# Setup work of the first phase put in another order: taps, LoRA B products, weight lo parts, and two bias loads

## The reference, cut to what matters

```
agg_w = einsum('bk,koi->boi', softmax(...), weight)
y     = einsum('boi,bih->boh', agg_w, x) + agg_b
z     = y @ A_eff.T,  A_eff = einsum('bn,nri->bri', gate, lora_A)   # and A_shared
x    += y @ kernel + bias + z @ B_eff.T                              # and B_shared
```

## Time and profile before

| what | us |
|---|---|
| three runs | 838.28, 838.53, 830.34 |
| the profiled execution, its own time | 831.89 |
| span of the profiled execution | 829.8 |
| TensorE busy in the span | 786.4 |
| VectorE, ScalarE, GpSimd busy | 532.7, 208.1, 88.3 |

### The profile page before, as it was taken

The page is one execution under the profiler, slowest core; times in us unless marked ns, Lnnn a source line. Parts: engine busy times, 40 slices in busy tenths (PEclk is TensorE's granted clock), DMA queues, the critical chain, the costliest instruction groups (busy, mean ns, idle before and its releaser), DMA issues.

```text
span 829.8 us, 10413 instructions
## 1 busy us (share of the span) xinstructions
PE 786.4 (95%) x3889; PEld 659.2 (79%) x3889; DVE 532.7 (64%) x634; ACT 208.1 (25%) x251; POOL 88.3 (11%) x59
## 2 busy tenths in 40 slices
PE   5998889999999999789999999999999989999998
PEld 4867678888888999668888877877778868888886
DVE  4855775264443479987777759766665795565552
ACT  4431101010010032233333326332233641111110
POOL 4440532323222000000000000000000000000000
PEclk9999999999999999899999999999999999999999
DMA  8966845455455896244455232277754764444441
GB/s 277 238 180 188 216 109 132 122 119 135 111 143 127 199 279 194 70 126 127 126 159 145 76 127 77 64 200 206 203 163 177 271 236 152 153 152 152 167 161 76
DMA packets 88379, 131.45 MB, mean 158 GB/s; under 512 B 11208, under 2 KB 66936, under 8 KB 85656
## 3 DMA queue, kind: packets, MB, share of 16 engines
q1 hardware_dynamic: 85136, 129.90, 53.4%
q10 hardware_dynamic: 3064, 0.90, 0.7%
q0 software_dynamic: 144, 0.21, 0.1%
HBM read 78.20 MB, written 51.72 MB: 157 GB/s over the span
## 4 chain that ended last, share of the span: by engine, by line
PE 72%; DVE 10%; DMA 8%; SPq 5%; issue 3%; ACT 2%; DVEq 0%; ACTq 0%
PE ps L1561 30%; PE ps L1804 25%; PE ps L1862 16%; DMA w_raw<-in_L_ffn_w 2%; DVE cr L1279 1%; DVE cf L1271 1%; SPq L438 1%; DMA w_scratch<-w_d 1%; SPq L592 1%; DMA x<-x_scratch 1%; DVE w_s_lo L1252 1%; DMA lora_b_scratch<-lb_c_lo 1%; DMA h_f<-h_scratch 1%; SPq L355 1%; DMA res<-r_scratch 1%
## 5 line engine op out<-in xcount | busy, mean ns | idle before, releaser
L1804 PE MATMUL ps<-cr,w_s_hi 128*128 128x512 f32 x512 | 159.5, 393 | 5.1 <-ACT s L915 4.9
L1804 PE MATMUL ps<-cr,w_a_hi 128*128 128x512 f32 x384 | 122.2, 400 | 10.7 <-DVE s L1357 6.0
L1804 PEld LDWEIGHTS ps<-cr,w_s_hi 128*128 128x128 f32 x512 | 96.5, 189 | 27.2 <-issue 4.0
L1804 PE MATMUL ps<-cr,w_s_lo 128*128 128x512 f32 x256 | 100.2, 391 | 0.0
L1804 PEld LDWEIGHTS ps<-cr,w_a_hi 128*128 128x128 f32 x384 | 73.3, 192 | 28.4 <-DVE s L1357 8.1
L1561 PE MATMUL ps<-wk_hi,y_hi 128*128 128x512 f32 x256 | 80.5, 395 | 0.3 <-issue 0.3
L1561 PE MATMUL ps<-wk_lo,y_hi 128*128 128x512 f32 x256 | 79.0, 390 | 0.0
L1561 PE MATMUL ps<-wk_hi,y_lo 128*128 128x512 f32 x256 | 78.9, 389 | 0.0
L1127 DVE TENSOR_TENSOR x_t<-ps,x_t 128x1024 f32<-128x1024 f32 x16 | 19.6, 1222 | 92.3 <-PE ps L1561 92.3
L741 POOL TENSOR_TENSOR x_t<-x_in,f_bias 128x1024 f32<-128x1024 f32 x16 | 63.3, 3960 | 143.0 <-DMA x_scratch<-x_t 143.0
L1499 DVE TENSOR_TENSOR res<-ps,res 128x512 f32<-128x512 f32 x56 | 38.6, 689 | 59.0 <-PE ps L1862 58.3
(11 more groups left out here) (176 smaller groups left out, 1255.4 us busy)
## 6 DMA issues: line engine op xcount, KB each, us to landing
x_scratch<-x_t SPq DMA_DIRECT2D x128, 64.5 KB, 2.1
x<-x_scratch SPq DMA_DIRECT2D x32, 258.0 KB, 7.4
x_in<-in_x SPq DMA_DIRECT2D x16, 512.0 KB, 5.3
r_scratch<-r_t SPq DMA_DIRECT2D x16, 512.0 KB, 3.1
raw<-in_L_ffn_w SPq DMA_DIRECT2D x64, 128.0 KB, 4.7
h_scratch<-s SPq DMA_DIRECT2D x32, 256.0 KB, 2.4
h_f<-h_scratch SPq DMA_DIRECT2D x8, 1024.0 KB, 5.9
res<-r_scratch SPq DMA_DIRECT2D x16, 512.0 KB, 5.0
```

The source lines that it names most:

```text
L1804: last = pe.matmul(o, l, r, start=first and q == 0 and n == 0, stop=q == 3 and n == 2, skip_group_check=True)
```

## The change

1. `wpad` is made on VectorE ahead of the four `mix_t` copies, `turn_taps` follows the first y on TensorE, and ScalarE copies the taps after LoRA A's first hi part.
2. LoRA B's products move forward on TensorE: results 0 and 1 ahead of u's step 3, results 2 and 3 ahead of step 4.
3. `POOL_WK` shrinks from (0, 1, 2) to (0,): VectorE makes seven lo parts. The lo parts of LoRA B move ahead of those of weight rows 6 and 7.
4. ScalarE issues the eight b12 loads after y's splits of tile 3, not between the hi parts of weight rows 5 and 6.
5. Three buffers change places: LoRA B's first lo tile to 90 KB, the b3 row to 199.75 KB, the first r tile to 90 KB. So the b3 load waits for weight row 7's slot and stands behind `first_group_lb` in SyncE's queue, and ScalarE waits for the r stores before it writes convolution parts.

```diff
-                for n, ks in (("hi", (162.25, 186.25)), ("lo", (199.75, 203.75)))]
+                for n, ks in (("hi", (162.25, 186.25)), ("lo", (90, 203.75)))]
...
-        r_t = [at(f"r_t{s}", [P, NL], 199.75 + 4 * s) for s in range(2)]
-        b3_s = at("b3_s", [P, NL], 90)
+        r_t = [at(f"r_t{s}", [P, NL], k) for s, k in enumerate((90, 203.75))]
+        b3_s = at("b3_s", [P, NL], 199.75)
...
-        POOL_WK = (0, 1, 2)
+        POOL_WK = (0,)
...
             load_wk(7)
-            wait_slot(sp, raw_of(5))
-            sp.dma_start(b3_s[:, :], b3.partition_broadcast(P)).then_inc(b3_in, 16)
             sp.wait_ge(lbs_made, 2)
...
             first_group_lb(sp, 0)
+            wait_slot(sp, raw_of(7))
+            sp.dma_start(b3_s[:, :], b3.partition_broadcast(P)).then_inc(b3_in, 16)
             sp.wait_ge(lora_taken, N_LORA)
...
             la_hi_part(0)
+            act.wait_ge(taps_mm, 1)
+            for half in range(2):
...
+            last.then_inc(taps_made, 1)
             split_y(1, 0, 1)
...
                 act.dma_start(f_bias[:, :], f0_bias.partition_broadcast(P)).then_inc(fbias_in, 16)
-                for m in range(4):
-                    for h in range(2):
-                        act.dma_start(b12_s[32 * m:32 * m + 32, h, :],
...
             wk_hi_part(6)
             wk_hi_part(7)
-            act.wait_ge(taps_mm, 1)
...
             split_y(3, 1, 1)
+            with nc.allow_non_contiguous_dma(reason="a few columns of small arrays"):
+                for m in range(4):
+                    for h in range(2):
+                        act.dma_start(b12_s[32 * m:32 * m + 32, h, :],
...
+            act.wait_ge(r_stored[0], 16 * TILES // 2)
...
+            dve.wait_ge(wpad_zeroed, 1)
+            dve.wait_ge(small_in, 48)
+            dve.tensor_copy(wpad[:, 8:8 + TAPS, :], w9_raw[:, :, :].rearrange("o c k -> o k c")).then_inc(wpad_made, 1)
             for q in range(4):
...
             y_rest(0, 0, 0)
-            dve.wait_ge(wpad_zeroed, 1)
-            dve.wait_ge(small_in, 48)
-            dve.tensor_copy(wpad[:, 8:8 + TAPS, :], w9_raw[:, :, :].rearrange("o c k -> o k c")).then_inc(wpad_made, 1)
+            wk_lo_part(1)
...
-            take_y(1, 0, 1)
+            add_bias(1)
+            wk_lo_part(2)
+            y_rest(1, 0, 1)
             wk_lo_part(3)
...
             wk_lo_part(5)
+            for n in range(4):
+                lb_lo_part(n)
             wk_lo_part(6)
             wk_lo_part(7)
-            for n in range(4):
-                lb_lo_part(n)
...
             y_tile(0, 0, 16, True)
+            turn_taps()
             small_turns()
...
             first_u(0, 1)
+            pe.wait_ge(taps_made, 1)
             la_result(2)
...
                 first_u(1, k)
-            for k in range(3, 5):
-                dst, dst1 = first_u(0, k), first_u(1, k)
-            turn_taps()
             lb_result_mm(0)
             lb_result_mm(1)
-            dst, dst1 = first_u(0, 5), first_u(1, 5)
-            pe.wait_ge(taps_made, 1)
+            dst, dst1 = first_u(0, 3), first_u(1, 3)
+            pe.wait_ge(lora_taken, 4)
             lb_result_mm(2)
             lb_result_mm(3)
-            for k in range(6, 8):
+            for k in range(4, 8):
                 dst, dst1 = first_u(0, k), first_u(1, k)
```

More of the change, by code:

```diff
@@ L833, in _ @@
             la_hi_part(0)
+            act.wait_ge(taps_mm, 1)
+            for half in range(2):
+                last = act.activation(taps[:, :, half, :].rearrange("p g (q o) -> p g q o", q=PH),
+                                      bank(6 + half).rearrange("p (q g o) -> p g q o", q=PH, g=GRP), ACT.Copy)
+            last.then_inc(taps_made, 1)
             split_y(1, 0, 1)
@@ L844, in _ @@
                 act.dma_start(f_bias[:, :], f0_bias.partition_broadcast(P)).then_inc(fbias_in, 16)
-                for m in range(4):
-                    for h in range(2):
-                        act.dma_start(b12_s[32 * m:32 * m + 32, h, :],
-                                      b12.rearrange("(h m j b) -> h m b j", h=2, m=4, j=NJ)[h, m]).then_inc(b12_in, 16)
             wk_hi_part(6)
             wk_hi_part(7)
-            act.wait_ge(taps_mm, 1)
[L852 to L855, removed]
             for n in range(4):
@@ L860, in _ @@
             split_y(3, 1, 1)
+            with nc.allow_non_contiguous_dma(reason="a few columns of small arrays"):
+                for m in range(4):
+                    for h in range(2):
+                        act.dma_start(b12_s[32 * m:32 * m + 32, h, :],
+                                      b12.rearrange("(h m j b) -> h m b j", h=2, m=4, j=NJ)[h, m]).then_inc(b12_in, 16)
             for k in range(4, 6):
@@ L1632, in turn_taps @@
                 pe.wait_ge(wpad_made, 1)
-                pe.wait_ge(lora_taken, 4)
                 for half in range(2):
```

## The result

The changed kernel takes 829.41 us (median of 20 runs, 825.13 to 831.96), the kernel before on the same chips 833.55 us (20 runs, 828.3 to 838.53). The ratio is 0.9945, with a 95% interval of 0.9926 to 0.9964: 4.6 us faster by the ratio, 4.1 by the medians, where the forecast was 1.9 us slower and 837 us. One execution in this document, the third of run e10, took 2783 us and is left out of that run's numbers. The profiled execution's own time is 827.55 us, against 831.89 before.

The account below looks back on a forecast made before the run. TensorE was taken as the bound, busy 786.4 of 829.8 us, with at most 12.3 us to win in three waits. Landing +0.9 and clock +1.0 gave +1.9 us on 834.8, so 837 us, range 827 to 844.

Parts of the forecast that it names:

- Early work: Moved taps and weight lo parts before about 61 us: hidden behind TensorE's work, taken as 0, bounds 0 and +1 us.
- LoRA B's lo parts about 6 us earlier: On VectorE, LoRA B's last lo part is made at 48.4 us, against 54.45 before.
- Wait 1: TensorE's 3.04 us wait for group 0's LoRA B copies goes, with its low clock: u of tile 2 ends 4.7 us earlier.
- Wait 2: TensorE's 2.77 us wait for group 1's LoRA B grows to 8.3 us; the last store lands 0.9 us later.
- +1.4 for the start: Term of the stores' landing: the DMA work from x of tile 3 on starts 1.4 us later, 49.7 against 48.34.
- "-2.2" for the copies: Term of the stores' landing: shared LoRA B copies finished before and ScalarE's copies ahead by 1.2 us, estimated at -2.2 us.
- rival C: Queues run freely: the last store lands at 72.5 us, wait 3's low clock goes; -8.1 us, 827 us; chance 0.10.
- Behind it: After wait 2 the clock falls; y of tile 4 comes 2 us later, about half returns: +1.0 us.
- wait 3: TensorE's 3.2 us "issue" wait for VectorE's y lo parts: forecast to stay at 2.5 us, its 1.6 us low clock too.
- B: Issues decide: landing 1.6 us earlier, VectorE 1.0 later, wait 3's low clock gone; -2.2 us, 833 us; chance 0.20.
- D: Slower: b3 ahead of the stores costs 4.8 us, later start, b12 and clock the rest; +8.2 us, 843 us; chance 0.12.
- E: ScalarE's group 0 copies queue behind the x loads and wait 1 stays; +0.9 us, 836 us; chance 0.08.

Follow-up runs that it names:

- e10: Changed kernel with GpSimd's first x plus bias of the loop held until VectorE has made y of tile 4 with its bias; 832.38 us, ratio 1.0006.
- e1: Changed kernel with the weight lo parts of k = 1 and 2 back on GpSimd; 829.26 us, ratio 0.9938 to the kernel before.
- e7: Changed kernel with LoRA B's four lo parts again behind those of weight rows 6 and 7 on VectorE; 828.53 us, ratio 0.9945.
- e2: Changed kernel with the b3 load behind the eight LoRA B stores in SyncE's queue; 829.58 us, ratio 0.9941 to the kernel before.
- e6: Changed kernel with LoRA B's DRAM laid out so each store has 64 rows of one stride, not 8 blocks of 8; 827.62 us, ratio 0.9907.
- e8: The e6 kernel plus GpSimd's third x plus bias held until VectorE has made y's lo parts of tile 5; 823.81 us, ratio 0.9902.
- e3: Kernel before with only GpSimd's x plus bias for tile 4i + 4 held until y's lo parts of tile 4i + 5 are made; 831.16 us, ratio 0.9958.
- e3b: Changed kernel with GpSimd's third x plus bias held until VectorE has made y's lo parts of tile 5; 828.29 us, ratio 0.9954.
- e5: Changed kernel with the eight b12 loads back between the hi parts of weight rows 5 and 6 on ScalarE; 831.46 us, ratio 0.998.

## Why the prediction was wrong

**Early work: no effect.** Right: y of tile 2 starts 41.3 us behind y of tile 0 in the changed kernel and in e1, 41.9 before.

**LoRA B's lo parts about 6 us earlier.** They end at 49.68, not 48.4, against 54.45; the difference to the forecast is that run's late start. The step was right but counted for less than I made of it: with them last again (e7) wait 1 stays gone.

**Wait 1: goes.** Right: 3.04 became 0.42 us, and u of tile 2 ends at 81.32, 2.35 us earlier (3.65 with the late start of that run taken off), where 4.7 was forecast. A part went to y of tile 3, which waits 1.67 us for the y bias, whose transfer took 10.5 us beside ScalarE's early copies, and to waits of 0.42 and 0.25 us in place of the 3.04. The forecast had no term for the bias.

**Wait 2: takes it all back.** Wrong in size: 3.4 us, not 8.3. TensorE arrives 2.3 us later than forecast (81.32, not 79.0), and goes on 2.6 us earlier (84.74, not 87.3). The landing of the last store moved by -2.2, not +0.9. By the terms: x of tile 3 is issued at 50.87, 2.5 later than before, of which 1.3 is that run's late start, so the +1.4 for the start holds. From there to the landing it takes 25.9 us, not 30.7: -4.8, where -2.2 + 1.7 = -0.5 was forecast. b3 is not the miss (e2 gives 2.4 for it). The miss is the "-2.2" for the copies that were out of the way: what is left for this term is -4.8 - 2.4 = -7.2. The last store is issued at 65.55, not 71.23, as rival C had it; it then lands 11.26 us later, not 7.82, as the bound by engines has it. I treated the busy half of the engines as busy without a gap from x of tile 3 on. It cannot have been, since the same transfers and b3 went through in 25.9 us; the share of 0.48 could not tell a full half from a queue that issues too slowly. How much of the -7.2 was such gaps and how much the shared copies, no run separates. That the stores themselves are bound by too few engines is right (e6: 6 us earlier). The Trainium skill, "DMA: Bandwidth & Descriptors", section on why a DMA increments its semaphore by 16, ties the number of engines to the outermost dimension; e6, where that went from 8 to 64 and the share to 1.01, agrees with it.

**Behind it: +1.0, and wait 3 stays.** This is the step that failed most. I read the low clock behind wait 2 as a cost of 2 us of which half returns. It cost 1.7 us of TensorE, and it came with an order of VectorE and GpSimd in which wait 3 and the low clock behind it are gone, 3.2 + 1.6 = 4.8 us. It made up 1.54 of the 2.09 us by which the order turned. The forecast kept wait 3 at 2.5 us because it treated the collision as a length that shrinks in proportion. It is a question of order. The addends were all in the trace: GpSimd alone takes 3.9 us for one addition, and VectorE's pair without it 1.3. The loser waits for a whole instruction: 0.65 + 3.8 + 0.65 = 5.1, measured 4.95. The Trainium skill, "SBUF — State Buffer", section "SBUF: two separate sides", says that the shared port pair is an exclusive lock, taken by whoever starts first for a whole instruction. The traces here agree: 4.95 where VectorE is first by 0.32 us, 6.93 where GpSimd is by 1.77, 8.62 where GpSimd is by 0.04 (e8), 1.29 where they miss each other. Carried through, it would have given the answer: VectorE first, residual blocked, tile 5 blocked; GpSimd first, none of it.

With the sizes of the runs: taking the collision out of the kernel before gives 3.5 us (e3), and putting it back into the changed kernel costs 5.1 us by the ratios and 3.0 by the medians of two batches (e10); by TensorE's progress it is 4.4 and 5.1 of 6.2. e1 is against it: there the collision is back in the profile and the time is not. What is left for waits 1 and 2 together lies between nothing and some 2 us: e3 and e3b, which both have no collision, are 0.3 us apart by their ratios, 1.0 by TensorE's progress and 2.9 by their medians. So "wait 2 takes back what wait 1 gives" was nearly right as a whole, and the gain came from a place at which the change does not touch a line. That 829.4 us lies in the range of 827 to 844 is no merit of the sum: the range's lower end was made for C.

Of the rivals, B (-2.2 us) and C (-8.1) lie on either side of the measured -4.6. B had the landing at -1.6, where it was -2.2, or -3.5 with the late start taken off; C had the issues running freely, which they did. But both let only the low clock of wait 3 go and not the wait. D and E did not happen.

## What to carry to other kernels

Where two engines lock each other out, ask who starts first and what each start hangs on, and follow the order through the next three instructions; here a lead of 0.3 us one way or the other went with 3 to 5 us of TensorE's time. Then fix the order with a wait of its own, before tuning the transfers in front of it: without the hold, each shorter wait 2 (e1, e5, e6) brought the collision back, and in e6 it hid a part of the gain. The stores that used half the DMA engines were better cured by their layout (e6) than by their place in the queue (e2). And take one profile's times with care: the same piece of work, untouched by any run, differed by up to 3.9 us between profiles.

## What the runs showed of the hardware that was not expected

- A low clock came with a gain. In the changed kernel, e2, e3b and e7 the clock fell to the lower of its two levels (1.2 GHz) in y of tile 4, which took 3.6 to 3.8 us instead of 2.05, and none of the four has wait 3. In the kernel before, e5 and e6 it stayed at 2.4 GHz, and all three have it; so has e1, where it fell only in part (2.56 us). That the low clock is what turned the order is worked out above and not shown by itself: no run changes the clock alone.
- How long TensorE had waited does not sort where the clock fell. It fell behind waits of 4.47 us (e3), 3.04, 3.2 and 3.42, but also behind 2.84 (e1, y of tile 3 took 2.48 us instead of 2.02), 2.45 (e5, 2.53 us) and 2.21 (e1, y of tile 4). It stayed at 2.4 GHz behind 2.77 us (before), 2.07 (e1), 1.96 (e5) and 1.48 (e6).
- VectorE's addition that reads PSUM (`x_t<-ps,x_t`) takes 1.21 us in the middle of GpSimd's pair (94.01 in the kernel before), the same as elsewhere; only its instructions with both inputs in SBUF were held up.
- Issuing the eight b12 loads of 1 KB took ScalarE 4.4 us early on and 8.1 us at 66 us, among the stores. Nothing waited for it there.
